# Reciprocal roots of the heads' variances on ScalarE and VectorE instead of GpSimd, in a fused decoder layer with routed experts

## The reference

```python
# layer 1: gated linear attention, 16 heads of 32 channels
o = scan(S = S * exp(log_sigmoid(kg) / 16) + k v^T ; o = q S)
o = (o - mean(o)) * rsqrt(var(o) + 1e-5)              # per head
x = x + (silu(gproj) * o) @ Wo.T
# layer 2: cross attention, 16 heads of 32 channels
q = ln(x @ Wq + bq) ; k = ln(y @ Wk + bk)             # per head, eps 1e-6
x = x + (softmax(q k^T) v + softmax(q k_dca^T) v_dca) @ Wo + bo
# layer 3: 4 experts, two per token, 512 tokens each
logits = layernorm(x) @ Wg + bg ; ... ; x = x + sum of the experts' outputs
```

## Time and profile before

| | |
|---|---|
| median of 3 runs | 1053.38 us (1051.97 to 1053.78) |
| the profiled execution's own time | 1052.63 us |
| its span, first to last instruction | 1050.9 us |
| busy share of the span | PE 89%, PEld 53%, DVE 66%, ACT 43%, POOL 47% |
| mean granted TensorE clock | 0.937 of full speed |

### The profile page before, as it was taken

One profiled execution on the slowest core, in us unless ns is written; L12 is line 12 of the kernel. 1 busy time (PEld: TensorE's weight loads), 2 busy tenths in 40 slices (PEclk: granted clock), 3 DMA queues, 4 the chain that ended last, 5 costly groups with the idle time before them and its releaser, 6 DMA issues.

```text
span 1050.9 us, 19085 instructions
## 1 busy us (share of the span) xinstructions
PE 932.2 (89%) x7297; PEld 559.8 (53%) x7297; DVE 697.7 (66%) x1293; ACT 453.1 (43%) x754; POOL 499.1 (47%) x563
## 2 busy tenths in 40 slices
PE   3688999999999999999999663069999999999995
PEld 1446666766666766776676442034444444444342
DVE  6767677878887788778886545856554445345672
ACT  3444555565566655665555423122232333233210
POOL 1447677767677777767775720111070001003643
PEclk9788999999999999999999965569999999999998
DMA  8413000000000000000000006032335234335593
GB/s 289 133 51 128 4 15 18 5 17 17 15 2 17 17 14 14 6 17 14 17 2 14 11 12 229 26 115 83 118 90 191 80 121 160 100 100 198 159 243 121
DMA packets 40300, 78.39 MB, mean 75 GB/s; under 512 B 11378, under 2 KB 11650, under 8 KB 40258
## 3 DMA queue, kind: packets, MB, share of 16 engines
q1 hardware_dynamic: 35266, 63.13, 18.0%
q0 software_dynamic: 4992, 14.70, 5.1%
HBM read 64.16 MB, written 13.65 MB: 74 GB/s over the span
## 4 chain that ended last, share of the span: by engine, by line
PE 74%; DVE 7%; POOL 5%; issue 4%; DMA 4%; SPq 3%; ACT 1%; POOLq 0%; DVEq 0%; ACTq 0%
PE ps L1009 18%; PE ps L1010 17%; PE ps L1011 17%; PE ps L1015 6%; PE ps L1102 4%; PE ps L1181 3%; PE ps L1197 3%; POOL y_fetched L728 2%; PE ps L1206 2%; POOL hrs L596 2%; PE ps L1226 2%; DVE big L1674 1%; DMA y_fetched<-y_scratch,idx_get 1%; SPq L473 1%; PE ps L1114 1%
## 5 line engine op out<-in xcount | busy, mean ns | idle before, releaser
L596 POOL TENSOR_TENSOR hrs<-hve,neg_half 128x16 f32<-128x16 f32 x48 | 140.2, 2921 | 3.8
L982 ACT ACTIVATE big<-ps 128x512 f32<-128x512 f32 x64 | 38.2, 597 | 233.2 <-PE ps L1011 233.0
L1771 DVE TENSOR_SCALAR big<-big 128x512 f16<-128x512 f32 x64 | 27.8, 435 | 110.4 <-ACT big L982 110.3
L1009 PE MATMUL ps<-w2h,big 128*128 128x512 f16 x256 | 97.0, 379 | 2.5 <-DVE big L1363 2.5
L1009 PE MATMUL ps<-big,w1h 128*128 128x512 f16 x256 | 97.8, 382 | 1.4 <-DVE big L1363 1.4
L1011 PE MATMUL ps<-big,w1l 128*128 128x512 f16 x256 | 97.8, 382 | 0.0
L1010 PE MATMUL ps<-big,w1h 128*128 128x512 f16 x256 | 97.8, 382 | 0.0
L1010 PE MATMUL ps<-w2l,big 128*128 128x512 f16 x256 | 97.0, 379 | 0.0
L1011 PE MATMUL ps<-w2h,big 128*128 128x512 f16 x256 | 97.0, 379 | 0.0
L711 POOL DMA_INDIRECT big<-x_scratch,token_of x16 | 18.3, 1147 | 149.3 <-PE ps L1015 77.5
L728 POOL DMA_INDIRECT y_fetched<-y_scratch,idx_get x32 | 37.5, 1173 | 104.8 <-DMA y_scratch<-big 89.4
(11 more groups left out here) (305 smaller groups left out, 2530.5 us busy)
## 6 DMA issues: line engine op xcount, KB each, us to landing
wst<-in_w SPq DMA_DIRECT2D x28, 1024.0 KB, 5.2
x_scratch<-xn SPq DMA_DIRECT2D x16, 256.0 KB, 2.1
y_fetched<-in_w SPq DMA_DIRECT2D x4, 1024.0 KB, 13.4
out<-x_all SPq DMA_DIRECT2D x4, 1024.0 KB, 7.9
pr<-in_w_attn SPq DMA_DIRECT2D x3, 1024.0 KB, 8.4
x_all<-in_w_attn SPq DMA_DIRECT2D x3, 1024.0 KB, 11.7
x_all<-in_x SPq DMA_DIRECT2D x1, 3072.0 KB, 11.7
y_scratch<-big SPq DMA_DIRECT2D x3, 1024.0 KB, 6.1
```

Source lines behind the costliest of these rows:

```text
L596: pool.tensor_tensor(hrs[n][:, :], hve[n][:, :], neg_half[:, :], ALU.pow).then_inc(hdev[n], 1)
L982: act.activation(hg[f % 2], psum[f % 2][:, 512:1024], ACT.Gelu, scale=UN).then_inc(hg_r, 1)
L1009: nc.tensor.matmul(o, lh, rh, start=first, stop=False)
```

## The change

The power on POOL goes. `head_deviation` becomes an ACT step of two instructions: a logarithm of the variance, with the epsilon added as a bias held in a column of `eps_head`, then an exponential with scale -0.5. Both functions are in the table set that is loaded at the start. `head_norm` on DVE gets three small instructions of 128 x 16 in front, one Newton step that refines the root; each waits for the one before. In the lists:

- ACT gets `head_deviation 1` behind `k_square`, `head_deviation 2` between `p_out 0` and `row_norm 0`, and `head_deviation 0` between `o_square` and `gate_sigmoid`; `x3_out` moves ahead of `row_norm 1`, and `logits_out` ahead of `x2_hi`.
- DVE has `head_var 1` ahead of `a1_gate` instead of behind it.
- PE does the expert logits (`b2_logits`) between the first two and the last two of the four blocks of `a1_g`, instead of after `b1_x`.

```diff
@@ buffers
-        hve = [sb(f"hve{n}", [P, HEADS]) for n in range(3)]
+        hln = [sb(f"hln{n}", [P, HEADS]) for n in range(3)]
-        eps_head = sb("eps_head", [P, 3, HEADS])
+        eps_head = sb("eps_head", [P, 3])
+        newton = [sb(f"newton{n}", [P, HEADS]) for n in range(3)]
@@ GpSimd
-                pool.memset(eps_head[:, n, :], DV * EPS_HEAD[n])
+                pool.memset(eps_head[:, n:n + 1], DV * EPS_HEAD[n])
-            def head_deviation(s, n):
-                b, par, half = s
-                after(pool, hv[n], b)
-                pool.tensor_tensor(hve[n][:, :], hvar[n][:, :], eps_head[:, n, :], ALU.add).then_inc(hdev[n], 1)
-                after(pool, hdev[n], b, nth=1, per=2)
-                pool.tensor_tensor(hrs[n][:, :], hve[n][:, :], neg_half[:, :], ALU.pow).then_inc(hdev[n], 1)
-                on(s[2], head_deviation, 1)
-                on(s[2], head_deviation, 2)
                 on(s[2], out_bias)
-                on(s[1], head_deviation, 0)
@@ ScalarE
+            def head_deviation(s, n):
+                b, par, half = s
+                after(act, hv[n], b, nth=1, per=4)
+                act.activation(hln[n][:, :], hvar[n][:, :], ACT.Ln, bias=eps_head[:, n:n + 1]).then_inc(hdev[n], 1)
+                after(act, hdev[n], b, nth=1, per=2)
+                act.activation(hrs[n][:, :], hln[n][:, :], ACT.Exp, scale=-0.5).then_inc(hdev[n], 1)
                 on(s[2], k_square)
+                on(s[2], head_deviation, 1)
                 on(s[1], gate_log)
                 on(s[2], q_square)
                 on(s[3], p_out, 0)
+                on(s[2], head_deviation, 2)
                 on(s[0], row_norm, 0, xn, xn_r)
...
                 on(s[1], o_square)
+                on(s[1], head_deviation, 0)
                 on(s[1], gate_sigmoid)
...
                 on(s[1], kv_out)
+                on(s[3], x3_out)
                 on(s[1], row_norm, 1, xn2, xn2_r)
                 on(s[0], ctx_hi)
-                on(s[3], x3_out)
+                on(s[3], logits_out)
                 on(s[1], x2_hi)
-                on(s[3], logits_out)
@@ TensorE
-                on(s[0], a1_g)
+                on(s[0], a1_g, range(KC // 2))
+                on(s[3], b2_logits)
+                on(s[0], a1_g, range(KC // 2, KC))
                 on(s[1], b1_x)
-                on(s[3], b2_logits)
@@ VectorE
             def head_norm(s, n, dst, src, done, scale=1.0):
                 after(dve, hdev[n], s[0], nth=2, per=2)
+                dve.scalar_tensor_tensor(newton[n][:, :], hvar[n][:, :], DV * EPS_HEAD[n], hrs[n][:, :], ALU.add, ALU.mult).then_inc(hv[n], 1)
+                after(dve, hv[n], s[0], nth=2, per=4)
+                dve.scalar_tensor_tensor(newton[n][:, :], newton[n][:, :], -0.5, hrs[n][:, :], ALU.mult, ALU.mult).then_inc(hv[n], 1)
+                after(dve, hv[n], s[0], nth=3, per=4)
+                dve.scalar_tensor_tensor(hrs[n][:, :], newton[n][:, :], 1.5, hrs[n][:, :], ALU.add, ALU.mult).then_inc(hv[n], 1)
+                after(dve, hv[n], s[0], nth=4, per=4)
                 dve.scalar_tensor_tensor(heads(dst[:, :]), heads(src), DV ** 0.5 * scale, per_head(hrs[n][:, :]), ALU.mult, ALU.mult).then_inc(done, 1)
...
+                on(s[2], head_var, 1, ksq)
                 on(s[1], a1_gate)
-                on(s[2], head_var, 1, ksq)
```

More of the change, by code:

```diff
@@ L1016, in turn, with rows @@
                 last.then_inc(done, 1)
-            def rows(ps, xh, xl, col, done, opens=True):
-                for k in range(KC):
+            def rows(ps, xh, xl, col, done, opens=True, ks=range(KC)):
+                for k in ks:
                     last = mm3(ps, xh[:, k, :], xl[:, k, :], wh[:, k, col:col + D], wl[:, k, col:col + D], opens and k == 0, k == KC - 1)
-                last.then_inc(done, 1)
+                if k == KC - 1:
+                    last.then_inc(done, 1)
             def second_kv():
@@ L1082, in a1_v, with a1_g @@
                 rows(a1, xth, xtl, C_V, v_ps)
-            def a1_g(s):
+            def a1_g(s, ks):
                 b, par, half = s
@@ L1087, in a1_g @@
                 after(pe, v_r, b)
-                rows(a1, xth, xtl, C_G, g_ps)
+                rows(a1, xth, xtl, C_G, g_ps, ks=ks)
             def a2_scores(s, rnd):
```

## The result

The changed kernel takes 1077.4 us (median of 4 runs, 1076.65 to 1078.15) against 1053.58 for the kernel before beside it (4 runs): a ratio of 1.0236, interval 1.0219 to 1.0254. It is slower, and the forecast of 1073.4 misses by 4 us, inside its own range. The profiled execution took 1077.66 with a span of 1075.9, so both grew by 25.0 us.

A forecast was written before the change was run, and what follows sets the result against it. The prediction took PE's own work in the full iterations as the bound; 11.7 + 7.8 + 1.3 + 0 = 20.8 us on 1052.63 gave 1073.4 us. Its own range was 1067 to 1082, the range with rivals 1060 to 1092.

The forecast's parts named there:

- The bound: In the full pipeline, 104 to 562 us, iterations of 34.18 us are PE's own work; POOL's power is expensive but hidden.
- Part A: From `b1_x` to `a1_turn`: PE stands still 0.96 us per iteration for `xn`, 11.7 us in all.
- the account of the swap: On the way to `xn`: the keys' head sum ahead of `gf` on DVE adds 0.60 us to the chain.
- Part B: DVE's stretch up to `otl`: three Newton instructions make `a2_wo` wait 0.60 us longer per iteration, 7.8 us in all.
- the upper end given: At `qraw`, ready within 0.1 us of PE's asking: nothing taken, 0.2 us as the upper end.
- Part C: Logits between the gate's halves on PE: switching between fp32 and fp16 matmuls costs 0.1 us per iteration, 1.3 us in all.
- Part D: Fill and drain: at most 8.4 us of waits given back; gain 1, loss 1, so nothing, ends -5 and +1.
- The clock: Rival: PE's new waits lower the clock once in each of 13 iterations, 22 us more, 1095; chance 0.08.
- The range: Own range of the whole forecast: 14 us more (1067) to 29.4 us more (1082).
- The faster rival: If ACT reaches `row_norm 0` within 7.27 us and DVE has 0.6 us spare, edge waits go: likely 1050; chance 0.10.

The follow-up runs named there:

- e1: The changed kernel without the three Newton instructions of each head norm on DVE: 1068.23 us, ratio 1.0111 to the kernel before.
- e3: The changed kernel with ACT's logarithm and exponential for the queries behind `row_norm 0` instead of ahead of it: 1067.08 us, ratio 1.0093.
- e7: The changed kernel with DVE's `a1_stats` behind the keys' sum and the gate's evacuation instead of ahead of them: 1067.62 us, ratio 1.0087.
- e4: The changed kernel with `head_var 1` on DVE behind `a1_gate` again, as before the change: 1098.26 us, ratio 1.0401.
- v1: The changed kernel with the queries' roots behind `xn` on ACT and the Newton step on POOL as six small instructions: 1052.18 us, ratio 0.9938.
- e5: The kernel before with only the logits moved between the halves of the gate, `x3_out` and `logits_out` moved along: 1060.99 us, ratio 1.0011.
- e2: The changed kernel with the logits behind `b1_x` again, `x3_out` and `logits_out` back in their places: 1085.0 us, ratio 1.0269.
- e6: The kernel before with the three Newton instructions on DVE added on top of POOL's power: 1112.03 us, ratio 1.0495.
- v3: v1 with the logits behind `b1_x` again: 1060.27 us, ratio 1.0026.

## Why the prediction was right, and where it wasn't

**The bound.** Right: before, an iteration is PE's own work, so every wait put into it counts 13 times. e1, e3 and e7 take the waits away one at a time, and the iteration shortens by 0.71, 0.42 and 0.77.

**Part A.** The chain came out as reckoned, in us behind the end of `b1_x`'s transposes (366.79): end of the gate's functions 5.55 forecast and 5.55 measured, of `q_square` 6.05 and 6.03, start of the logarithm 6.81 and 6.79, end of the exponential 7.38 and 7.35, end of `xn` 8.19 and 8.15. PE's idle time is 0.95 against 0.96. What it costs from step to step is 1.16, though, since matmuls that follow one another overlap and these no longer do; the weight load ahead of `a1_turn` stands idle for 1.18. The term should have been 13 x 1.16 = 15.1 instead of 11.7: the modelled end of a matmul is not the time at which the next could have started. The logarithm is 0.308 and the exponential 0.216, against 0.32 and 0.22. (With the durations that the prediction takes from the Trainium skill, 0.20 + 0.29, the estimate of the stall comes out 0.05 smaller, not 0.03.) What was wrong is the account of the swap: e4 shows that it saves 0.45, not that it costs 0.60.

**Part B.** Right: 0.59 against 0.60 per iteration, 7.7 against 7.8 us over the 13 iterations. e1 takes this away, and 0.07 at `a1_kg1` with it. The three instructions take 166, 174 and 175 ns and are 0.2 apart, and POOL was indeed idle beside all of them. What the part left out is their price at fill and drain: without them the routing starts 13.3 us earlier (e1), not 7.7. `kraw` was in time, `qraw` late by 0.07, within the upper end given. One thing has moved without changing the sum: POOL's product of `od` starts ahead of the scan now, so the scan takes 1.53 (0.69 before) and `dq` 0.43 (1.31 before), 1.96 together against 2.00.

**Part C.** The sign was wrong. The new order doesn't cost 0.1 but saves 0.27 per iteration, 3.5 us, as after, e1 and v1 show alike: the logits' step is 0.81 instead of 0.99 and that of `b1_x` 0.53 instead of 0.61. Why is not shown. But the cover it takes was rightly in part A; e5 and e2 show both sides.

**Part D.** Right in its sum: fill and drain together lost 0.8, where the forecast said nothing, with +1 as the upper end. The balance was another, though. Of the 8.4 us of rows 2, 3.0 are left, one wait of 2.0 for `od` among them, which was to vanish; and what was gained there went to the Newton step, 4.7 us by e1.

**The clock.** This is the term missing from the sum. I gave it as a rival with a fall in each iteration or in none, and it came in between: four more, 6 us. Without it, A's 3.4 too little and C's 4.8 too much nearly cancel (13 x 1.55 = 20.2 against 20.8), which is luck. The 4 us by which the forecast misses are about this term, less the 1.4 that the routing and the experts took less. The argument against the rival was that gaps under 1 us are small. The experiments answer that. With the logits between the halves, a wait for `xn` of 1.39 us has 11 stretches, one of 0.95 or 0.94 has 5 (after and e1), and one of 0.17 or less none (e3, e7, v1). With the logits behind `b1_x`, 8 came in e2, 5 in e6 and 2 in v3's shortest execution, at `b1_q` in all three. That the wait brings the falls behind `a1_turn` is shown by its removal in two ways, by ACT's order and by DVE's. The counts are of one execution each, but the mean clocks of all runs go the same way: 0.918 to 0.920 in e4, 0.928 to 0.934 in after and e1, 0.934 to 0.940 in e3 and e7. Why it is five iterations and not all, and why e2 has four times as many as the kernel before, which has the logits at the same place, stays open.

**The range.** Its ends were not added up as the parts gave them. Part B names 0.9 per iteration as its upper bound and the sum took 0.7; part D names -5 and the sum took -2. With the parts' own bounds the range is 1064 to 1085 instead of 1067 to 1082. The result lies in both.

**The faster rival.** It asked for ACT to reach `row_norm 0` in time and for 0.6 us in DVE's stretch. The change has neither; v1 makes both nearly so, by ACT's order and with the Newton step on POOL, and then what the rival named is what one gets: the edges' gain, and 0.6% less time.

## What to carry to other kernels

An instruction that waits for another engine costs, in a strict queue, what stands behind it: put the two-instruction root behind the step that feeds the bound engine, not where its own data are due. Work taken off an idle engine is worth nothing until its result was late; here it was late five times in all, and the replacement belongs on that same idle engine, as v1 has it. Sum a stall from matmul start to matmul start, and count, in the trace, the stretches of low clock as well as the waits, since a wait under 1 us can bring on one worth 1.5.

## What the runs showed of the hardware

- A wait of PE of 0.94 us in an iteration of 36 was followed, in 5 of 13 iterations, by 3.4 us at the lower clock; and the clock also fell with PE full, in a place that lay behind the logits and `a2_scores 0` (e2, eight times; e6, five times). The nine kernels with the logits in the middle of the gate had none there in their full iterations.
- A DVE instruction of 128 x 16 with two SBUF inputs took 0.94 to 1.25 us where it started while one of POOL's large products ran, and 0.16 to 0.19 elsewhere (e6). The one that starts second is the longer: in iteration 9 of the kernel before the scan started at 340.13, POOL's product at 340.17 and `dq` at 340.86, and they took 0.69, 1.72 and 1.31. In the changed kernel the product started at 351.79 and the scan at 352.08, and they took 1.27 and 1.53, with 0.43 for `dq`.
- The logarithm of 128 x 16 with a column as bias took 308 ns and the exponential with immediates 216. The Trainium skill, "ScalarE: Activation LUTs", section "What ACT_TABLE_LOAD costs", would give an estimated 0.29 and 0.20: it is right to 0.02.
